# Spreading the histogram's operations anew over the stages and turns of a sort

## The reference

```python
def gcn_conv(x, W, b, src, dst, n):
    h = x @ W
    s, d = concat([src, arange(n)]), concat([dst, arange(n)])   # self-loops
    deg = segment_sum(ones, d, n)
    dis = rsqrt(deg)
    return segment_sum(h[s] * (dis[s] * dis[d])[:, None], d, n) + b

g = relu(gcn_conv(service_emb, W1, b1, src, dst, 6250))         # 32 features
g = gcn_conv(g, W2, b2, src, dst, 6250)
ctx = g[context_idx].reshape(512, -1)                           # 3 rows each
y = concat([user_emb[user_idx], ctx], axis=1) @ fc_W + fc_b     # 512 x 6250
```

## Time and profile before

| | us |
|---|---|
| median of three runs (lowest, highest) | 770.29 (768.8, 771.91) |
| the profiled execution | 772.33 |
| its span, first to last instruction | 770.5 |
| VectorE busy in the span | 600.2 (78%) |
| TensorE matmuls busy | 587.4 (76%) |
| ScalarE busy | 422.5 (55%) |
| GpSimd busy | 182.4 (24%) |

### The profile page before, as it was taken

The page is one execution under the profiler, slowest core; times in us unless marked ns, Lnnn a source line. Parts: engine busy times, 40 slices in busy tenths (PEclk is TensorE's granted clock), DMA queues, the critical chain, the costliest instruction groups (busy, mean ns, idle before and its releaser), DMA issues.

```text
span 770.5 us, 21867 instructions
## 1 busy us (share of the span) xinstructions
PE 587.4 (76%) x9504; PEld 551.6 (72%) x9504; DVE 600.2 (78%) x1436; ACT 422.5 (55%) x770; POOL 182.4 (24%) x181
## 2 busy tenths in 40 slices
PE   0404662676929735478699999999999999997997
PEld 0304662675928725478699999999999998997643
DVE  9999999988999999787999999999984211111376
ACT  4993389797999111247588888888877000000000
POOL 1100000000000200377776666676200000000500
PEclk9999995978978965589899999999999999999999
DMA  7000000000000000235366665565200999859386
GB/s 127 2 0 1 1 1 1 1 2 1 2 3 2 5 0 1 58 92 173 100 211 209 209 209 205 183 204 199 66 3 3 359 414 408 289 153 303 86 316 284
DMA packets 39143, 94.13 MB, mean 122 GB/s; under 512 B 19097, under 2 KB 21843, under 8 KB 39044
## 3 DMA queue, kind: packets, MB, share of 16 engines
q1 hardware_dynamic: 24340, 74.28, 26.2%
q0 software_dynamic: 5216, 9.91, 6.1%
q10 hardware_dynamic: 9488, 8.52, 3.4%
HBM read 48.50 MB, written 44.18 MB: 120 GB/s over the span
## 4 chain that ended last, share of the span: by engine, by line
PE 55%; DVE 34%; issue 3%; ACT 3%; POOL 2%; DMA 1%; SPq 0%; DVEq 0%; POOLq 0%
PE pp L1430 17%; PE pp L1448 14%; PE psY L1448 13%; DVE arena L960 12%; DVE arena L961 11%; PE pp L1549 5%; PE psY L1346 3%; DVE arena L947 2%; POOL arena L655 2%; ACT arena L711 2%; PE pp L1366 1%; PE psX L1417 1%; DVE arena L958 1%; DVE arena L959 1%; DVE arena L955 1%
## 5 line engine op out<-in xcount | busy, mean ns | idle before, releaser
L1430 PE MATMUL pp<-arena 128*128 128x128 fp8e4 (+1 forms) x2401 | 189.4, 221 | 7.5 <-DVE arena L1140 6.3
L788 ACT ACTIVATE arena<-pp 128x512 uint16<-128x512 f32 x308 | 172.1, 584 | 42.0 <-PE pp L1430 39.7
L655 POOL DMA_INDIRECT arena<-ordered_keys,window x147 | 161.3, 1097 | 128.3 <-DMA ordered_keys<-arena 62.0
L711 ACT ACTIVATE arena<-arena,neg_word 128x780 fp8e4<-128x780 bf16 (+1 forms) x200 | 170.3, 942 | 10.4 <-PE psY L1346 10.4
L1430 PEld LDWEIGHTS pp<-arena 128*128 128x128 fp8e4 (+1 forms) x2401 | 148.4, 98 | 8.0 <-issue 6.0
L1448 PE MATMUL psY<-arena 128*128 128x96 bf16 x2401 | 150.5, 207 | 2.4 <-ACT y_s L772 2.1
L1448 PEld LDWEIGHTS psY<-arena 128*128 128x128 fp8e4 x2401 | 123.3, 98 | 2.9 <-ACT arena L788 2.6
L1139 DVE TENSOR_SCALAR arena<-arena 128x384 int32<-128x384 int32 (+5 forms) x224 | 110.8, 495 | 7.7 <-PE pp L1430 7.6
L1448 PE MATMUL pp<-arena 128*128 128x96 bf16 x2401 | 104.2, 206 | 9.0 <-issue 8.9
L1448 PEld LDWEIGHTS pp<-arena 128*128 128x128 fp8e4 x2401 | 102.7, 98 | 10.6 <-issue 10.5
L960 DVE TENSOR_TENSOR arena<-arena 128x832 f32<-128x832 f32 (+4 forms) x121 | 107.5, 889 | 3.1
(11 more groups left out here) (205 smaller groups left out, 543.6 us busy)
## 6 DMA issues: line engine op xcount, KB each, us to landing
arena<-adjacency_spill SPq DMA_DIRECT2D x32, 784.0 KB, 10.5
adjacency_spill<-arena SPq DMA_DIRECT2D x24, 768.0 KB
adjacency_spill<-arena SPq DMA_DIRECT2D x8, 832.0 KB
out_dram<-arena SPq DMA_DIRECT2D x12, 512.0 KB, 3.8
out_dram<-arena ACTq DMA_DIRECT2D x8, 512.0 KB, 3.8
arena<-adjacency_spill SPq DMA_DIRECT2D x8, 392.0 KB, 5.0
arena<-ordered_keys,window POOLq DMA_INDIRECT x147
arena<-in_L_rec_fc_b_dram SPq DMA_DIRECT2D x3, 784.0 KB, 12.1
```

The source lines that it names most:

```text
L655: nc.gpsimd.indirect_dma_start(gath[:, k, q, :], None, ordered, bass.IndirectOffsetOnAxis(ap=window[:, q, d:d + 1], axis=0)).then_inc(gat[ ...
L711: ins = nc.scalar.activation(cols8[n % BUFS][:, 4 * u:4 * u + 4, 0:c1 - c0], high4[:, :, c0:c1], ACT.Sign, bias=neg_word[:, u:u + 1], satu ...
L788: nc.scalar.mul(adj16[g % SLOTS][:, m0 * P:m1 * P], bank(gp)[:, 0:(m1 - m0) * P], PAIR_SCALE).then_inc(evicted, 1)
L1430: ins = MM(bank(gp)[:, (n - n0) // 2 * P:((n - n0) // 2 + 1) * P], src_hot(h, n - a), dst_hot(h, n - a), start=n % 2 == 0, stop=n % 2 == 1 ...
```

## The change

It changes when units, words and tiles are issued, and splits the clamps; the operations themselves are the same, 64 units, 200 words and 1563 tiles.

- Units: two batches (16 units) instead of one (8) are issued in the stages before turn 0, the first eight one a stage in stages 1 to 8, the next eight two in three stages up to stage 20. The others are spread over turns 0 to 12 (`HIST_END` = `DONE_TURN` - 2) instead of 0 to 11.
- Words: in proportion to the stages up to stage 96, without the first 50 apart.
- Tiles: for each batch a begin is worked out (after its units and words are planned, at 24 tiles a stage), and each turn's block ends where that count stands then, in the middle of a batch if need be. Before, a block ran to the end of a batch where it could.
- The caps by room in the buffers stay and are asserted.
- Clamps: the four user indices at turn 6, the twelve context indices at turn 8, instead of both at turn 12. The last instruction of each signals `clamped`; GpSimd's gathers of context rows wait for the second.
- `earlier_rows` stays at turns 13 and 14, now named by `DONE_TURN`.

What the two plans give, turn by turn (units, words and tiles issued at that turn; units in stages before turn 0 apart: 8 before, 16 after):

| turn | before stage | units before, after | words before, after | tiles before, after |
|---|---|---|---|---|
| 0 | 28 | 5, 4 | 50, 59 | 195, 281 |
| 1 | 29 | 5, 4 | 3, 2 | 0, 24 |
| 2 | 36 | 4, 4 | 17, 14 | 195, 85 |
| 3 | 38 | 5, 3 | 4, 5 | 0, 38 |
| 4 | 45 | 5, 4 | 17, 14 | 0, 157 |
| 5 | 48 | 0, 4 | 7, 6 | 86, 0 |
| 6 | 55 | 8, 1 + clamps | 17, 15 | 109, 158 |
| 7 | 59 | 0, 6 | 9, 8 | 108, 37 |
| 8 | 66 | 8, 2 + clamps | 17, 15 | 87, 134 |
| 9 | 71 | 7, 5 | 12, 10 | 195, 61 |
| 10 | 78 | 5, 3 | 17, 15 | 195, 134 |
| 11 | 84 | 4, 5 | 14, 12 | 0, 61 |
| 12 | 91 | clamps, 3 | 16, 15 | 195, 158 |
| 13 | 98 | 0, 0 | 0, 10 | 195, 75 |
| 14 | 105 | 0, 0 | 0, 0 | 3, 160 |
| 15 | 113 | 0, 0 | 0, 0 | 0, 0 |

The diff, cut to its core:

```diff
-EARLY_WORDS, WORDS_BY = 2 * WORDS, 91
+WORDS_BY = 96
-EARLY_UNITS, EARLY_BY = UNITS, 20
+EARLY_UNITS = 2 * UNITS
+TILES_A_STAGE, TILES_LEAD = 24, 10
...
-        HIST_END = DONE_TURN - 3
+        HIST_END = DONE_TURN - 2
+        CLAMP_TURNS = (6, 8)
...
         def units_by(stages, turns):
-            early = min(EARLY_UNITS, -(-EARLY_UNITS * stages // EARLY_BY))
+            early = min(EARLY_UNITS, stages if stages <= UNITS else UNITS + (stages - UNITS) * 2 // 3)
             return early + -(-(NBATCH * UNITS - EARLY_UNITS) * min(turns, HIST_END + 1) // (HIST_END + 1))
...
+        def words_by(stages):
+            return min(NBATCH * WORDS, -(-NBATCH * WORDS * stages // WORDS_BY))
+
+        def written_at(n):
+            return next(s for s in range(STAGES) if units_by(s, sum(t < s for t in TURN_STAGES)) >= UNITS * (n + 1)
+                        and words_by(s) >= WORDS * (n + 1))
+
+        begun, free = [], 0
+        for n in range(NBATCH):
+            c0, c1 = batch_cols(n)
+            start = max(free, written_at(n) * TILES_A_STAGE + TILES_LEAD)
+            begun.append((start, c0, c1))
+            free = start + c1 - c0
+        tiles_by = [max([min(c1, c0 + t * TILES_A_STAGE - start) for start, c0, c1 in begun if t * TILES_A_STAGE > start] or [0])
+                    for t in TURN_STAGES[:DONE_TURN + 1]]
...
+            pool.wait_ge(clamped, 2)
             for k in range(4):
                 pool.wait_ge(table_out[k], 16 * len(range(k, NG, 4)))
...
-            def clamp_indices():
+            def clamp_indices(part):
+                lo, cnt, src, dst, size = ((0, BB, uidx[:], ucl[:], USERS), (BB, BB * CTX, cidx[:].rearrange("p b c -> p (b c)"), ccl[:], N))[part]
                 dve.wait_ge(heads_in, 32)
...
-                dve.sem_inc(clamped, 1)
+                V.tensor_copy(dst, f).then_inc(clamped, 1)
...
-                if turns == HIST_END + 1:
+                if turns in CLAMP_TURNS:
                     dve.wait_ge(weights_in, 16 * (GC + 1 + 2 * CTX))
-                    clamp_indices()
-                elif turns == HIST_END + 2:
+                    clamp_indices(CLAMP_TURNS.index(turns))
+                elif turns == DONE_TURN - 1:
                     earlier_rows((NQ2 - 1,))
-                elif turns == HIST_END + 3:
+                elif turns == DONE_TURN:
                     earlier_rows(range(NQ2 - 1))
```

More of the change, by code:

```diff
@@ L454, in gcn_kernel @@
         LAST_TURN, DONE_TURN = TURNS - 1, TURNS - 2
-        HIST_END = DONE_TURN - 3
-        def share_of(total, turn_weight, stages, turns):
-            end = TURN_STAGES[HIST_END] + turn_weight * HIST_END
-            return min(total, -(-total * (stages + turn_weight * turns) // end))
+        HIST_END = DONE_TURN - 2
+        CLAMP_TURNS = (6, 8)
         def units_by(stages, turns):
-            early = min(EARLY_UNITS, -(-EARLY_UNITS * stages // EARLY_BY))
+            early = min(EARLY_UNITS, stages if stages <= UNITS else UNITS + (stages - UNITS) * 2 // 3)
             return early + -(-(NBATCH * UNITS - EARLY_UNITS) * min(turns, HIST_END + 1) // (HIST_END + 1))
[L466 to L474, removed]
+        def words_by(stages):
[11 more added lines that the diff above has]
+                    for t in TURN_STAGES[:DONE_TURN + 1]]
         def room_at(turn):
@@ L484, in words_ready_by @@
         def words_ready_by(stages, turns):
[L485 to L493, removed]
+            return min(words_by(stages), WORDS * room_at(min(turns, DONE_TURN)))
+        for k, counted_then in enumerate(tiles_by):
+            needed = sum(c0 < counted_then for _, c0, _ in begun)
+            assert units_ready(TURN_STAGES[k] - 1, k) >= UNITS * needed and words_ready_by(TURN_STAGES[k], k) >= WORDS * needed
         assert tiles_by[-1] == USED
@@ L961, in exchange @@
                 return V.tensor_tensor(o_high, low, high, ALU.max)
-            def clamp_indices():
+            def clamp_indices(part):
+                lo, cnt, src, dst, size = ((0, BB, uidx[:], ucl[:], USERS), (BB, BB * CTX, cidx[:].rearrange("p b c -> p (b c)"), ccl[:], N))[part]
                 dve.wait_ge(heads_in, 32)
[L965 to L971, removed]
-                dve.sem_inc(clamped, 1)
+                f, g = idx_f[:, lo:lo + cnt], neg_f[:, lo:lo + cnt]
+                link(V.tensor_copy(f, src))
+                link(V.tensor_scalar(g, f, 0.0, float(size), ALU.is_lt, ALU.mult))
+                link(V.tensor_tensor(f, f, g, ALU.add))
+                link(V.tensor_scalar(f, f, 0.0, float(size - 1), ALU.max, ALU.min))
+                V.tensor_copy(dst, f).then_inc(clamped, 1)
             def glue(part):
```

## The result

The changed kernel took 768.13 us (median of 13 runs), the kernel before in the same measurement 772.87 (13 runs): a ratio of 0.9932, interval 0.9905 to 0.9958. One of the 13 runs of the changed kernel took 3176.41 us and is left out of the ratio. Measured twice more, beside other kernels, the ratio was 0.9912 [0.9883, 0.9941] and 0.9915 [0.9885, 0.9945]. The mean of the three, 0.9920, is 6.2 us of 773.6. The forecast was a ratio of 763.1 / 770.29 = 0.9907 and a time of at most 767.5: the forecast ratio lies inside all three intervals, the mean gain came out a little smaller, and the time lies outside the range.

What follows compares the result with a forecast made beforehand. VectorE's time in the sort (29.2 to 314 us) was taken as the bound. The terms 6.9 + 0.9 - 0.35 - 0.3 gave 7.15, say 7.2 us less, turning 770.29 into 763.1; the range ran from 760 to 767.5.

Steps and rivals of the forecast that it cites:

- The split I made: VectorE's 6.9 us of sort waits: turns 5 and 7 lack filler, turns 6 and 8 are a knot of buffers.
- signs of being wrong: VectorE waiting over half a microsecond before turns 1, 12 or 13, tiles over 80 ns, or early sort without early gather.
- Term 4: TensorE's tile blocks before the sort's transposes, at 66 ns a tile: large ones hide with 2.6 to 3.4 us to spare.
- Term 1: VectorE's idle time at turns 5 to 8 and behind the clamps goes, filled by units and clamps: 6.9 us.
- Term 2: Eight more units in stages 1 to 20 instead of turns, 0.36 against 0.475 us each: 0.9 us gained.
- Turn 3: In the sort, ScalarE's five words end after VectorE is through with three units: 0.2 to 0.5 us of new wait.
- Turn 13: 38 tiles wait for ScalarE's last ten words, transposes may run slowly: between nothing and 1.4 us lost, 0.3 taken.
- Turn 1: 24 tiles make its transposes 0.6 to 1.0 us late, but four units cover that: 0 to 0.1 us of wait.
- Turn 12: In the sort, ScalarE's words end before the copies are needed, with 0.6 us of cover, the smallest of the turns compared.
- Covers too short: Rival, chance 0.16: TensorE's small blocks and ScalarE's tight places come late, 3.5 us instead of 0.65; time 766 to 767.
- Nothing gained: Rival, chance 0.07: the rest does not wait for the sort's end, or idle time only moves to other turns; 770.3 us.
- Slower, by counting at the low clock: Rival, chance 0.07: TensorE's six large blocks before transposes run at 128 ns a tile, 38.8 us late, 802 us.

## Why the prediction was right or wrong

**The base.** The predicted 763.1 started from 770.29, the median of three runs. Thirteen runs had 772.87, and later comparisons 773.67, 773.64 and 774.28. Two of those three lie below every one of the 54 later runs of the kernel before in these comparisons (770.7 us and more), so they had been fast by chance. The result is 5.0 us above the forecast: this step put it 2.6 us up, and the gain, 4.7 us in that comparison instead of 7.2, another 2.4. I had allowed 2 us for the spread downwards and none upwards, although the profiled execution itself, 772.33, stood 2.0 above that median.

**The mechanism.** In the main it held. VectorE's busy time is the same to 0.4 us; its waits fell; ScalarE's words wait for no tile; the first user gather is at 159.58 us (forecast: near 159) and the first block of tiles at 48.71 (48). The split I made, two waits for want of filler and two from a knot of buffers, does not stand: with only the tile plan changed all four went (4.8 of the 6.6 us), so all four hung on the knot. Two of my own signs of being wrong were met: waits of over half a microsecond at turn 13 (1.1, first profile) and turn 1 (0.9, third), and tiles of over 80 ns in the small blocks. The waits in the sort were to be under 1 us in all; they were 1.9, 0.9 and 1.8.

**The step that failed besides the base** is the price of the new waits, 0.65 us in the sum and 0.7 to 1.7 measured. Term 4 counted tiles at the mean of long blocks and took the 2.6 to 3.4 us of cover in front of the transposes as safe. The runs showed that a stretch in which TensorE stands can bring the granted clock down to 0.50 (1.92 us of it at turn 12 in the first profile, 2.05 at turn 6 in the third), and what that costs at the next small block or transposes changes from one execution to the next.

**Terms of the sum,** at the sort's end, where 7.2 was forecast and 6.0, 7.5 and 6.4 were measured (313.20, 313.43 and 313.24 less the changed kernel's three values):

- Term 1, idle time that goes: 6.9 less 0.65 of new waits forecast. VectorE's waits went from 7.1, 7.4 and 7.0 us to 1.9, 0.9 and 1.8, so 5.6 in the mean.
- Term 2, units moved into stages: 0.9 forecast. The run with eight fewer says 1.3; the one unit beside the memset took back 0.47, so 0.8. The rule of the Trainium skill against it, that a semaphore costs nothing extra (VectorE: DVE Perf Modes, The DRAIN you can't avoid), is not borne out here: the units cost 0.35 us in a stage and 0.49 in a turn.
- Turn 3: forecast 0.2 to 0.5, measured 0.2. The reason was ScalarE's five words, and the run with words by stage 91, which has four there, shows no wait.
- Turn 13: I took 0.3 from a bound of 0 to 1.4; measured 1.1, 0.2 and 0.2. The reasons were the two named, late tiles and slow transposes; the size is one of chance.
- Turn 1: forecast 0 to 0.1; measured 0, 0.3 and 0.9. Here the step failed that took 66 ns for every tile behind slow transposes: the 24 tiles took 90, 106 and 115 ns. A block of 86, which I had read the earlier trace rows, shows only its mean of 69. Large blocks hid this, the smallest did not.
- Turn 12: cover of 0.6 us forecast for ScalarE. The copies were not late; but TensorE's transposes were slow in the first profile, 2.82 us after 1.92 us of standing, which I had counted as a fast turn: a wait of 0.4 there. The same happened at turn 6 in the third, 3.01 us after 2.05, where I had named no risk. At turns 8 and 10 of the first profile they were fast, 1.64 and 1.58 us, after 1.9 us.
- The memset: not foreseen. The earlier trace rows was the only row of GpSimd that I had weighed.

**Behind the sort.** I had taken every microsecond saved there to reach the end. The three profiles of the changed kernel took 458.8 to 460.3 us from the sort's end on, those of the kernel before 456.7 to 458.3. Three parts vary from profile to profile, whatever the kernel: the first layer (its last pair 282.1 to 287.1 us after the sort's end, over all 14 profiles), the second layer (111.4 to 117.3 us from there) and the last matmuls (47.2 to 50.4 us). In the first profile of the changed kernel TensorE's granted clock fell to 0.50 as the last matmuls began, and the first 16 took 8.80 us; in that of the kernel before it did not, and they took 7.11. The kernel before, then the changed one:

```profile
723.22 7.11 PE L1549 MATMUL pp<-arena 128*128 128x512 f32 x16 [0.53 <-DVE arena L1289]
```

```profile
718.49 8.80 PE L1550 MATMUL pp<-arena 128*128 128x512 f32 x16 [0.53 <-DVE arena L1290]
```

All three profiles of the kernel before have the short form, 47.2 to 47.3 us; of the changed one two have the long form, 48.9 and 49.0, and one the short form, 47.3. The seven variants of the changed kernel took 458.0 to 460.5 us behind the sort, the kernel before with only the new tiles, whose sort also ends 4.8 us earlier, 455.6. Whether the change makes this part longer or chance did it is open: the ratios (6.2 us in all, by an interval of some 2 us to either side each) allow both nothing and 2 us of loss. A kernel that only delays everything behind the sort by some microseconds would tell; it was not run.

**The rivals.** Covers too short (0.16) came true in part: most waits came at its named places, turns 1, 3, 12 and 13, and one at turn 6, which it had not named, others in each execution, 0.7 to 1.7 us without the one at turn 15 instead of the forecast's 0.65. Nothing gained is excluded by all three intervals. Slower, by counting at the low clock: the six large blocks took 64 to 81 ns a tile in the three profiles, and none of them was late; in the first TensorE stood 1.9 to 4.6 us between each and its transposes.

## What to carry to other kernels

Where fillers of a critical engine also feed a double buffer on two other engines, look first at where the buffer is given free: spreading the consumer's work (here the tiles) untied most of the waits, and let the filler through to turns that had none, before any rule for filler was changed. Cost a short block of matmuls behind a standstill by the first microseconds of a block, not by a long block's mean (here 69 to 115 ns a tile against 64), and give every hole in front of a critical transpose a price for slow tiles and slow transposes. Take the base from more runs than three, and when one phase is changed, compare its end in the trace: that repeated to 0.3 us for the kernel before and to 1.2 for the changed one, where whole times differed by several.

## What the hardware showed that I had not expected

TensorE's clock comes up at different times in executions of the same kernel. In the changed kernel, behind the slow transposes of turn 0 (from 90.6 us on, without a pause), the granted clock is 0.70 in 94 to 95 us in the first profile, and still 0.50 in 95 to 96 us in the third. The windows of TensorE, those of the first profile, then of the third:

```profile
94.00:95.00 1.00, 1.00 (x15) 0.70 0.00 0
95.00:96.00 1.00, 1.00 (x16) 1.00 0.00 0
```

```profile
95.00:96.00 1.00, 1.00 (x12) 0.50 0.00 0
96.00:97.00 1.00, 1.00 (x9) 0.68 0.00 0
```

Turn 1 waits 0 us in the first profile and 0.9 in the third. Over eight profiles with these 24 tiles, among them the variants above, the tiles take 69 to 115 ns each, the less the earlier the clock is up. VectorE and the transposes start alike in the first and the third; TensorE had stood 7.34 us before the transposes in the one, 7.90 in the other and 8.37 in the second, whose clock came up between the two, so the length of the standing does not order them. And a VectorE instruction of one input and one output beside a GpSimd memset took 1.02 instead of 0.56 us, while exchanges of two inputs beside the same memset took no longer than elsewhere.
